# A decoder layer's fourth feed-forward pass: another split of the integer product between GpSimd and VectorE, and two of ScalarE's conversions made by VectorE

## The reference, cut to what matters

```
def act_qdq(x):                        # 16-bit levels, one step for the WHOLE tensor
    scale = max(max(|x|) / 32767, 1e-12)
    return clip(round(x / scale), -32768, 32767) * scale

x    = act_qdq(layernorm(x))
up   = act_qdq(x @ lpbq_dequant(w_up).T)       # 128 -> 384
gate = act_qdq(x @ lpbq_dequant(w_gate).T)     # 128 -> 384
sig  = fixed_qdq_u16(sigmoid(gate))
gate = act_qdq(gate * sig)
o    = act_qdq(gate * up)                      # <- the product of this change
return o @ lpbq_dequant(w_down).T              # 384 -> 128
```

## Time and profile before

| | |
|---|---|
| median of 3 runs | 323.65 us (323.5 to 324.08) |
| the profiled execution's own time | 323.5 us |
| its span, first to last instruction | 321.7 us |
| TensorE (PE) | 298.0 us busy, 93% of the span |
| VectorE (DVE) | 271.2 us, 84% |
| ScalarE (ACT) | 255.3 us, 79% |
| GpSimd (POOL) | 193.0 us, 60% |
| granted clock of TensorE | 1.0 in this stage |

### The profile page before, as it was taken

How to read it: one execution, slowest core, us unless ns; L and a number is a source line. 1 busy time by engine, 2 the same in 40 slices (tenths; PEclk the granted TensorE clock), 3 DMA queues, 4 the chain that set the end, 5 groups by cost and what they waited for, 6 DMA issues and landing times.

```text
span 321.7 us, 10009 instructions
## 1 busy us (share of the span) xinstructions
PE 298.0 (93%) x3765; PEld 206.2 (64%) x3765; DVE 271.2 (84%) x653; ACT 255.3 (79%) x470; POOL 193.0 (60%) x340
## 2 busy tenths in 40 slices
PE   6999999999999999999999999899967789699996
PEld 5687877788566666666666666844322254359996
DVE  5489988789889989999999965877789996998763
ACT  3578888987899989999899887787787758994930
POOL 3679999982358796876848578100177773784000
PEclk9999999999999999999999999999999999999999
DMA  6851366652103656400000000000000000000134
GB/s 170 278 145 34 101 195 197 204 175 84 35 4 117 184 167 186 115 4 4 4 5 2 5 2 2 3 0 0 0 0 1 0 3 0 0 0 3 45 94 123
DMA packets 23754, 21.65 MB, mean 67 GB/s; under 512 B 3577, under 2 KB 21530, under 8 KB 23706
## 3 DMA queue, kind: packets, MB, share of 16 engines
q1 hardware_dynamic: 22170, 20.73, 21.4%
q10 hardware_dynamic: 1536, 0.28, 0.5%
HBM read 14.70 MB, written 6.30 MB: 65 GB/s over the span
## 4 chain that ended last, share of the span: by engine, by line
PE 53%; DVE 22%; ACT 8%; issue 8%; POOL 7%; ACTq 1%; POOLq 0%; DVEq 0%
DVE nm L1641 8%; PE banks L1025 8%; PE banks L1095 7%; PE banks L669 6%; DVE mxs L1869 6%; PE banks L795 5%; PE banks L739 5%; PE banks L630 4%; PE banks L662 3%; ACT ng L1402 2%; PE banks L817 2%; PE banks L732 2%; PE banks L716 2%; POOL rstd L400 2%; DVE mxs L1753 2%
## 5 line engine op out<-in xcount | busy, mean ns | idle before, releaser
L1641 DVE TENSOR_REDUCE nm<-banks 128x4 f32<-128x512 f32 x128 | 81.6, 680 | 6.3 <-PE banks L739 5.8
L1296 ACT ACTIVATE PT<-banks,bmask,vmask 128x1024 f32<-128x1024 f32 x64 | 76.8, 1202 | 0.1
L1025 PE MATMUL banks<-X3T,upT 128*128 128x512 f32 x96 | 44.3, 601 | 11.4 <-DVE mxs L1869 8.9
L599 POOL TENSOR_TENSOR G<-ng,sq 128x1536 int32<-128x1536 int32 (+3 forms) x10 | 27.9, 2793 | 36.3 <-DVE sq L1900 36.3
L1869 DVE TENSOR_REDUCE mxs<-G 128x1 f32<-128x1536 int32 (+5 forms) x32 | 42.4, 1345 | 4.2 <-ACT G L1363 3.8
L739 PE MATMUL banks<-kd,qd 32*128 32x128 f16 x512 | 39.3, 217 | 2.8 <-DVE nm L1641 2.5
L795 PE MATMUL banks<-PT,VP 128*32 128x128 f32 x1024 | 41.2, 279 | 0.5 <-ACT PT L1296 0.5
L1025 PEld LDWEIGHTS banks<-X3T,upT 128*128 128x128 f32 x96 | 17.4, 191 | 34.2 <-issue 15.8
L739 PEld LDWEIGHTS banks<-kd,qd 32*128 32x128 f16 x512 | 23.8, 92 | 20.3 <-DVE nm L1641 10.5
L1136 ACT ACTIVATE h<-X,shift,rstd 128x128 f32<-128x128 f32 x64 | 26.3, 483 | 7.5 <-POOL shift L445 7.4
L795 PEld LDWEIGHTS banks<-PT,VP 128*32 128x32 f32 x1024 | 24.1, 109 | 11.5 <-ACT PT L1296 5.3
(11 more groups left out here) (200 smaller groups left out, 728.1 us busy)
## 6 DMA issues: line engine op xcount, KB each, us to landing
kd<-k_dram SPq DMA_DIRECT2D x32, 128.0 KB, 2.6
qd<-q_dram SPq DMA_DIRECT2D x32, 128.0 KB, 2.7
ctxg<-in_ctx_dram SPq DMA_DIRECT2D x8, 256.0 KB, 3.0
out_dram<-y SPq DMA_DIRECT2D x7, 256.0 KB, 2.3
X<-in_x_dram SPq DMA_DIRECT2D x3, 512.0 KB, 6.8
X3T<-m_dram SPq DMA_DIRECT2D x1, 896.0 KB, 5.3
k_dram<-khi SPq DMA_DIRECT2D x7, 128.0 KB, 1.7
k_dram<-klo SPq DMA_DIRECT2D x7, 128.0 KB, 1.8
```

The lines of the kernel that those rows point to most:

```text
L599: nc.gpsimd.tensor_tensor(GI[:, c], ng[:, u, part], sq[:, u, part], ALU.mult).then_inc(S["b_t"], 1)
L1025: m = pe.matmul(bank(2 + FC * (g % 2) + k), w[:, k * P:k * P + P], grp(X3T, g), start=True, stop=True)
L1296: act.activation(PT[:, a, :], bank(2 + 2 * a, 2), ACT.Exp, bias=bmask[:, n:n + 1], scale=vmask[:, n:n + 1]).then_inc(S["t_exp"], 1)
L1641: V.tensor_reduce(nm[:, n % 2, c:c + NSET], bank(u).rearrange("p (h m) -> p h m", m=P), AX.X, ALU.max, negate=True).then_inc(S["t_max"], 1)
```

## The change

Three things change, all in the fourth pass:

1. `product_split` is gone. GpSimd takes the first 1024 columns (`SPLIT`) in every group, where it took 768 in groups 0 to 2, and VectorE takes 512, where it took 768. Group 0's gated levels are cut at 512 and 1024 columns instead of 768 and 768. The wait of GpSimd for VectorE's part in groups 0 to 2 stays.
2. In groups 4 and 6 (`LEVELLED`; the fifth and the seventh) ScalarE no longer makes the levels of the third block in PSUM. VectorE makes them, in the same place, with a `tensor_scalar` multiplication of 512 columns right ahead of its own product, and waits for its result (`c_ud`).
3. The counts of `c_un` follow (`up_made`).

```
+        LEVELLED = (4, 6)
+        SPLIT = 2 * GT
-        def product_split(g):
-
-            return PB if g < UW else 2 * GT
         def up_made(g):
-            return g + 1 if g < UW else 2 * g - UW + 2
+            return sum(1 if k < UW or k in LEVELLED else 2 for k in range(g + 1))
 # GpSimd
             for g in range(NG - 1):
-                u, w = g % 2, product_split(g)
+                u, w = g % 2, SPLIT
                 pool.wait_ge(S["c_tn"], g + 2)
                 pool.wait_ge(S["c_un"], up_made(g))
                 if g < UW:
                     pool.wait_ge(S["c_od"], g + 1)
 # ScalarE
-            silu_levels(0, slice(PB, FW))
-            silu_levels(0, slice(0, PB))
+            silu_levels(0, slice(SPLIT, FW))
+            silu_levels(0, slice(0, SPLIT))
...
             for g in range(UW, NG - 1):
-                if g > UW:
-                    up_levels_in_place(g, slice(product_split(g), FW))
-                up_levels(g, slice(0, product_split(g)))
+                if g > UW and g not in LEVELLED:
+                    up_levels_in_place(g, slice(SPLIT, FW))
+                up_levels(g, slice(0, SPLIT))
                 silu_levels(g, slice(0, FW))
 # VectorE
+            def up_levels_in_place(g, part):
+                dve.wait_ge(S["c_u"], g + 1)
+                V.tensor_scalar(up_bank(g).bitcast(I32)[:, part], up_bank(g)[:, part], lev[:, 2:3], None, ALU.mult
+                                ).then_inc(S["c_ud"], 1)
...
-                dve.wait_ge(S["c_un"], up_made(g) - (g >= UW))
+                if g in LEVELLED:
+                    up_levels_in_place(g, slice(SPLIT, FW))
+                    dve.wait_ge(S["c_ud"], 1 + LEVELLED.index(g))
+                else:
+                    dve.wait_ge(S["c_un"], up_made(g) - (g >= UW))
                 dve.wait_ge(S["c_tn"], g + 1 + (g > 0))
-                product(g, slice(product_split(g), FW))
+                product(g, slice(SPLIT, FW))
```

More of the change, by code:

```diff
@@ L236, in decoder @@
             b_u b_umx b_ng b_sig b_sq b_t b_mx
-            c_u c_un c_tn c_op c_od c_mx
+            c_u c_un c_ud c_tn c_op c_od c_mx
             d_oq d_on d_y d_yc d_st0 d_st1""".split()
@@ L1073, in _ @@
                 else:
-                    whole = product_split(g - 2) // GT
-                    hidden(g, upT, range(whole))
+                    hidden(g, upT, range(2))
                     pe.wait_ge(S["c_od"], g - 1)
-                    hidden(g, upT, range(whole, FC)).then_inc(S["c_u"], 1)
+                    hidden(g, upT, range(2, FC)).then_inc(S["c_u"], 1)
                 if g == 0:
@@ L1411, in _ @@
             act.wait_ge(S["g_lev"], 4)
-            silu_levels(0, slice(PB, FW))
-            silu_levels(0, slice(0, PB))
+            silu_levels(0, slice(SPLIT, FW))
+            silu_levels(0, slice(0, SPLIT))
             silu_levels(1, slice(0, FW))
-            up_levels_in_place(UW, slice(product_split(UW), FW))
+            up_levels_in_place(UW, slice(SPLIT, FW))
             silu_levels(2, slice(0, FW))
             for g in range(UW, NG - 1):
-                if g > UW:
-                    up_levels_in_place(g, slice(product_split(g), FW))
-                up_levels(g, slice(0, product_split(g)))
+                if g > UW and g not in LEVELLED:
+                    up_levels_in_place(g, slice(SPLIT, FW))
+                up_levels(g, slice(0, SPLIT))
                 silu_levels(g, slice(0, FW))
```

## The result

The changed kernel takes 324.74 us (median of 21 runs, 324.43 to 326.37) against 323.65 us for the kernel before (21 runs). The ratio is 1.0042 with a 95% interval of 1.0031 to 1.0053: 1.0 to 1.7 us slower. The medians differ by 1.09 us. Both kernels have some runs about 1.6 us above the rest, 4 of 21 before and 6 of 21 after; without these the medians still differ by 1.09. The forecast was 324.6, slower by 1.0. The profiled execution took 324.57 us and its span is 322.7 us; 324.5 and 322.7 had been worked out.

The account below looks back on a forecast made before the run. The pass was taken to end on TensorE's idle queue, with VectorE's unbroken tail 0.28 us behind it in slack. 0.51 (ping-pong) + 0.72 (conversion) - 0.23 (slack) = 1.0 us slower: 324.6 us, likeliest range 324.2 to 325.0.

Parts of the forecast that it names:

- The ping-pong: Groups 0 to 2: GpSimd's and VectorE's products take turns, so the wider GpSimd part ends 0.75 us later, 0.51 counting.
- ScalarE's saving: Groups 4 and 6: two conversions fewer, 0.57 us each start to start, first becoming a wait, worth nothing in the end.
- The conversion in the tail: Group 6's conversion on VectorE, ahead of its product where nothing absorbs it: 0.72 us later.
- TensorE's slack: At the pass's end TensorE's idle queue hides 0.28 us of VectorE's lateness, less 0.05 hand-over: 0.23 off the loss.
- The missing block: Rival, groups 0 to 2: narrower VectorE product not blocked, or GpSimd starts straight on; 323.3 us, chance 0.13.
- the cheap conversion: Rival, groups 4 and 6: VectorE's conversion takes 0.43 us instead of 0.69; 324.3 us, chance 0.12.
- the dear one: Rival, groups 4 and 6: VectorE's conversion reading and writing PSUM takes 0.95 us; 325.1 us, chance 0.10.
- The clock: Rival: TensorE's longer idle stretch in group 5 halves its clock, 14 idle products take 6.6 us; 328 us, chance 0.03.

Follow-up runs that it names:

- e1: Changed kernel with only the 1024/512 split, ScalarE making all levels as before; 324.23 us against 323.48 for the kernel before, ratio 1.0016.
- e5: Changed kernel with VectorE writing the levels of groups 4 and 6 to SBUF instead of PSUM; 326.85 us, ratio 1.0102 to the kernel before.
- e3: Changed kernel with group 6's conversion back on ScalarE, only group 4's on VectorE; 323.93 us, ratio 1.0004 to the kernel before.
- e4: Kernel before with group 4's conversion on VectorE and nothing else; 323.35 us, ratio 0.9993 to the kernel before.
- e9: e4 with group 2's third block kept in PSUM and GpSimd taking 1024 columns there; 326.14 us, ratio 1.0085 to the kernel before.
- e10: e9 without the last six idle products on TensorE; 326.14 us, ratio 1.0082 to the kernel before.
- e11: e9 with 12 idle products between group 4's second and third block, 2 instead of 6 ahead of group 5; 323.82 us, ratio 1.0008.
- e6: Kernel before without the last six idle products ahead of the transpose; 323.74 us, ratio 1.0005 to the kernel before.

## Why the prediction was right

**The ping-pong.** GpSimd's product 2 was to end 0.75 us later than before; it ends 0.73 later. The product of group 1 on VectorE was to end 0.53 behind GpSimd's product 0; it is 0.56. Group 0's product on GpSimd was to be released by ScalarE's levels, no longer by VectorE; it is. This step was tested alone in e1 (+0.50 where +0.5 to +0.6 was expected), and its cause in e5.

**ScalarE's saving.** Its levels of group 4 were to start at 281.03 and of group 6 at 286.54; with the 0.09 they start at 281.01 and 286.52. It waits 0.49 us where I had 0.6; the trace counts the wait from the end of the up levels, the forecast counted it from 1.00 behind their start, 0.09 before that end. That nobody needs group 6's levels earlier held: in e3, where ScalarE makes that conversion, VectorE is through with its maxima at the same time (20.20 us into the stretch, 20.21 in the changed kernel). Against e1, e3 also shows that the saving at group 4 is worth nothing beside the new widths, and e4 that it is worth 0.25 beside the old ones.

**The conversion in the tail.** The price was the one number with wide bounds, 0.427 to 0.744 us. It is 0.75, just outside the upper one, and 0.79 from its start to the product's with the wait. I had 0.72. This is the term that was mis-sized most, by 0.07. The product of group 6 starts at 290.57 (with the 0.09), forecast 290.51; the maxima are spread at 295.95, forecast 295.88. The rule of the Trainium skill on the doubled rate (VectorE: DVE Perf Modes, "Mode 2×_2P"), by which the cheap bound was dropped, was borne out in its direction: with only the source in PSUM the conversion takes 0.74 (e5), against the 0.427 of the earlier trace rows with both sides in SBUF. Where the prediction counts four maxima in the tail there are five, one at 290.00 and four from 291.20; its sum took their time from the rows and doesn't hang on the count.

**TensorE's slack.** I took 0.28 less 0.05, that is 0.23. Measured by what arrives at the step it is 0.17 (0.59 to 0.42). With the conversion's 0.07 this makes the stretch 1.12 instead of 0.99, and the 0.09 that the pass began earlier brings the span back to exactly 1.0. So part of the agreement to 0.1 us is luck; the mechanism isn't.

**The rivals.** The missing block and the cheap conversion are ruled out by the rows above. So is the dear one: its 0.95 us came from no row, and the conversion that reads and writes PSUM takes 0.75. The clock did not fall in the changed kernel (granted clock 1.00 in every stretch from 270 to 296 us). My estimate that TensorE's idle time ahead of group 5's third block grows to 2.1 us was wrong: it is 1.29, where it was 1.27, since VectorE's product of group 3, which ends it, comes only 0.20 later and TensorE's work ahead of it is 0.18 later too. The danger named there was real: e9 met it at 4.09 us, and e5 at 2.17 us, hardly more than the 2.07 us of the third pass that was held against it.

## What to carry to other kernels

Before work is moved from one engine to another, ask of each instance where the receiving engine stands at that moment: the same conversion, 0.79 us of VectorE's time, cost 0.63 in its tail, nothing beside a GpSimd that was the bound, and gave back 0.25 where ScalarE was it. Where two engines wait for each other in turn, as they do here, the sum of both durations counts, and a split that gives more to the one that is slower per column (2.37 us for 1024 columns on GpSimd, 0.69 for 512 on VectorE) makes it longer. And where a wait is put into TensorE's queue, look how long it will stand and what filler stands behind that same wait.

## What the runs showed that I had not expected

- TensorE, idle for 4.09 us, came back at a granted clock of 0.68 (e9) and 0.50 (e10) over the next three to four microseconds. Idle for 2.17 us in e5, it had 0.71 over the next 5.80. Idle for 2.07 us in the third pass and 1.43 in e11 it stayed at 1.00 (in the third pass from 241.4 to 244.4 us too, behind the gap, where the earlier trace rows ends at 241). What else sets the 2.17 of e5 apart from the 2.07 of the third pass isn't shown.
- A transpose that finds TensorE idle starts 0.15 us behind its releaser (e6), and 0.05 where TensorE was still at work on idle products (the changed kernel). So cutting the filler in front of it gave 0.11 us, not the 0.2 by which the queue overlapped.
- VectorE's scaled conversion of 512 columns from PSUM takes 0.74 to SBUF and 0.75 to PSUM, more than a two-input product with one input in PSUM (0.69).
- Blocked by VectorE, GpSimd's product took 2.69 us for 2.37 (e5, one case): the exclusion works both ways.
